# Two attention blocks and two Fourier blocks on one core: a job's projection, second norm and MLP placed among the attention steps of the next job

## The chip, the cores and the metric

The kernel runs on one core of one Trainium2 chip. The metric is device time in microseconds (us) from the start to the end of the one launch, taken as the median of several runs; lower is better.

## The reference, cut to what matters

Four blocks follow one another on an image batch of 8 x 16 x 16 x 192 (batch, height, width, channels), all in float32. The first two are windowed attention blocks with an MLP (the window is 14 x 14 and the image is padded to 28 x 28, so each image has four windows, three of them mostly padding). The last two go through the Fourier domain.

```
h = layernorm(x) * w + b                      # over the 192 channels
q, k, v = split(windows(h) @ qkv_w + qkv_b)   # 12 heads of 16 channels
a = (q / 4) @ k.T + rel_h(q) + rel_w(q)       # relative position terms, by row and by column
o = softmax(a) @ v
x = x + unwindow(o @ proj_w + proj_b)
h = layernorm(x) * w2 + b2
x = x + gelu(h @ up_w + up_b) @ down_w + down_b      # 192 -> 768 -> 192
# blocks 3 and 4
x = x + irfft2(softshrink(mix2(relu(mix1(rfft2(x))))))   # block-diagonal complex mixes
```

## The kernel before, in words

**Jobs, units and steps.** The batch is cut into four pairs of images (512 tokens each) and the two attention blocks are two layers, which makes eight *jobs*, numbered n = 0 to 7: job n is pair n % 4 in layer n // 4. A job's attention has nine *units* (three groups of four heads, times three kinds of windows: the full windows of image one, those of image two, and the cut ones, which the code calls window 2), and a unit has four heads, so a job has 36 *steps*. In a step TensorE makes the scores of a head that is some steps ahead (`scores`, L829), VectorE takes the row maximum (`row_max`, L435), and, for the head of this step, TensorE makes the transposed scores with the maximum already subtracted (`scores_T`, L869), ScalarE takes the exponential (`exps`, L617). The maxima of a unit are transposed on TensorE (`transpose_max`, L855), copied on VectorE (`copy_max`, L448) and put into a row of `q_aug` by a DMA that ScalarE issues (`send_max`, L660; two DMAs for a full window, one for a cut one). Once a unit's four exponentials are there, `values` (L885) multiplies them with v.

**The front of a job** is what comes before its attention: the first norm's transposes `transpose_x` (x), the projections to q and k in two groups of six heads, g = 0 and 1 (`project`, q and k), the relative terms (`bias`, 16 small matmuls, and `transpose_bias`, for each group and each axis; the program calls them h, H, w, W) and v (`values_in`). Each result is split into a high and a low part: ScalarE writes the high part (`q_high`, `k_high`, `r_high`), then VectorE the low one (`q_low`, `k_low`, `r_low`). Then SyncE (SP) sends them into the rows of `q_aug` and `k_aug` by DMAs within SBUF: for each group of six heads four of 192 KB for q, four of 192 KB for k, four of 168 KB for the relative terms (`send_keys` L238, `send_queries` L251, `send_bias` L258, and the loop `send` L275).

**The back of a job** is what follows its attention: transposes of the attention's output (`transpose_out`), the output projection (`project_out`), the residual sum and second norm on VectorE and GpSimd, `transpose_y`, the MLP's first product in six blocks (`up`, L939), gelu on ScalarE (L655), the second product (`down`, L951) and the sum to x. Gelu and exp need different tables of ScalarE: a dummy activation (`warm`, L673) makes the switch at a place of the program's choice.

**Order.** Every engine's program is written out by hand and runs in order. In the main loop over units u and heads e the 36 steps hold `scores` 12 heads ahead, `scores_T`, `values`, and group 0 of the next job's front at fixed steps (`X_SLOT`, `Q_SLOT`, `K_SLOT`, `R_SLOT`). After the 36 steps comes a stretch without steps: group 1 of the next front and the back of this job, in turns; the first 12 `scores` of the next job stand between the matmuls of `down`. In this document A is the stretch from the first to the last exponential of a job, and B the stretch from there to the first exponential of the next job.

**Banks.** PSUM has eight banks. Banks 0 and 1 hold scores, 2 and 3 transposed scores, 4 the values, 5 the small transposes, and 6 and 7 the front, in turns: the list `FRONT` gives each use its bank, and `front_free` (L755) makes TensorE wait until the use two places earlier has been read. The back uses banks 0 to 4, as no attention runs then. The MLP's hidden values lie in the memory of the exponentials `PT`. The weights of both layers have their own memory, loaded early.

Of the kernel before, what the change touches and what calls it, by code (L numbers as in the profile page):

```python
# [11 lines left out]
PAIRS = B // 2  # L12
# [15 lines left out]
RK = WS * HG  # L28
MLP = 4 * C
# [7 lines left out]
HEADS = 4 * UNITS  # L37
EARLY = 12
LAST = UNITS - 1
# [4 lines left out]
INV = [1.0 / 16, 1.0 / 256]  # L44

# [9 lines left out]
def window(u):  # L55
    return u % 3


def slot(n, u):
    return (UNITS * n + u) % 4  # L60


def head(i):
    return 4 * (i // 12) + i % 4
# [6 lines left out]
def front_uses(n):  # L71
    uses = ["x0", "x1", "q0", "k0"]
    if first_of_layer(n):
        uses += ["p0"]
    uses += ["h0", "H0", "w0", "W0", "q1", "k1"]
    if first_of_layer(n):
        uses += ["p1"]
    return uses + ["h1", "H1", "w1", "W1", "v0", "v1", "v2", "v3"]


FRONT = [(n, use) for n in range(JOBS) for use in front_uses(n)]
PROJ_BANK = (0, 1, 4, 2)
UP_BANK = (4, 3)
DOWN_BANK = (2, 4, 3, 2)
X_SLOT, Q_SLOT, K_SLOT, R_SLOT = 3, 8, 12, (18, 24)
BIAS_ORDER = ("h a w", "w h a")
V_TILES = [(0, 1), (2, 3), (4, 5), (6,)]


def front_bank(n, use):  # L90
    return 6 + FRONT.index((n, use)) % 2

# [33 lines left out]
def attention(nc, d, x_all, bank, consts):  # L126
    with ExitStack() as ctx:
# [3 lines left out]
        def sem(name):  # L131
# [6 lines left out]
        w_proj = [sb(f"w_proj{l}", [97, G, C]) for l in range(2)]  # L138
        w_up = [sb(f"w_up{l}", [96, G, MLP]) for l in range(2)]
        w_down = [sb(f"w_down{l}", [128, MC, C]) for l in range(2)]  # L140
        b_up = [sb(f"b_up{l}", [128, MC]) for l in range(2)]
        b_down = [sb(f"b_down{l}", [128, C]) for l in range(2)]
# [24 lines left out]
        spare = sb("spare", [1, 2])  # L167
        hidden = PT[:, :, :].rearrange("p s m -> p (s m)")[:, 0:MC * TOK].rearrange("p (m k) -> p m k", m=MC)
# [8 lines left out]
        PER = dict(stats1=1, stats2=1, aggr1=1, aggr2=1, veps1=1, veps2=1, rstd1=1, rstd2=1, xn1=1, xn2=1, xT_mm=2,  # L177
                   xT_dve=1, xT_act=1, q_mm=2, q_hi=2, q_lo=2, q_nat=2, k_mm=2, k_hi=2, k_lo=2, r_tok=4, rt_copy=4, r_mm=4, r_hi=4, r_lo=4,
                   v_mm=4, v_copy=4, s_mm=HEADS, max=HEADS, nt_mm=UNITS, negT=UNITS, st_mm=HEADS, exp=HEADS,
                   pv=UNITS, o_copy=UNITS, ot_mm=3, inv_sum=3, o_tok=3, oT_mm=2, oT_dve=1, oT_act=1, proj=4, x1=4, x1b=1,  # L180
# [9 lines left out]
        q_in = [sem(f"q_in{g}") for g in range(G)]  # L190
        k_in = [sem(f"k_in{g}") for g in range(G)]
        p_in = [sem(f"p_in{g}") for g in range(G)]
# [4 lines left out]
        Q_DMA, K_DMA, P_DMA = 16 * 8, 16 * 4, 16 * 4  # L197
        LD_FRONT, LD_BACK, LD_STATIC = 16 * 4, 16 * 7, 16 * 3

        def need(eng, name, n, k):  # L200
            if n >= 0:
                eng.wait_ge(S[name], n * PER[name] + k)

        def neg_count(n, u):
            U = UNITS * n + u
            return 16 * sum(1 if window(k % UNITS) == 2 else 2 for k in range(U % 4, U + 1, 4))

        def columns(u):
            return (CUT0, CUT) if window(u) == 2 else (WIN * window(u), WIN)
# [5 lines left out]
        def _(sp):  # L215
# [13 lines left out]
            def load_back(l):  # L229
                load(w_proj[l][0:96, :, :], d["proj_w"][l].rearrange("(g p) n -> p g n", g=G), ld_back[l])  # L230
                load(w_proj[l][96:97, 0, :], d["proj_b"][l].rearrange("(a n) -> a n", a=1), ld_back[l])
                load(b_down[l][:, :], d["down_b"][l].rearrange("(a n) -> a n", a=1).broadcast_to([128, C]), ld_back[l])
                load(b_up[l][:, :], d["up_b"][l], ld_back[l])
                load(w_up[l][:, :, :], d["up_w"][l].rearrange("(g p) n -> p g n", g=G), ld_back[l])
                load(w_down[l][:, 0:3, :], d["down_w"][l].rearrange("(g p) n -> p g n", g=MC)[:, 0:3, :], ld_back[l])
                load(w_down[l][:, 3:6, :], d["down_w"][l].rearrange("(g p) n -> p g n", g=MC)[:, 3:6, :], ld_back[l])

            def send_keys(n, g):  # L238
                need(sp, "st_mm", n - 1, 4 * (6 if g == 0 else UNITS))
                need(sp, "k_lo", n, g + 1)  # L240
                for z in range(2):
                    for r in (z, z + 2):
                        load(k_aug[r:BIAS:4, HG * g:HG * g + HG, 0:TOK].bitcast(F32), st_k[:, g, z, :].bitcast(F32), k_in[g])
                if first_of_layer(n):
                    sp.wait_ge(S["p_lo"], 2 * layer(n) + g + 1)
                    for z in range(2):
                        for r in (z, z + 2):
                            load(k_aug[r:BIAS:4, HG * g:HG * g + HG, TOK:KEYS].bitcast(F32),
                                 st_p[:, g, z, :].bitcast(F32), p_in[g])

            def send_queries(n, g):  # L251
                need(sp, "st_mm", n - 1, 4 * (6 if g == 0 else UNITS))
                need(sp, "q_lo", n, g + 1)
                for z in range(2):
# [28 lines left out]
            for n in range(JOBS):  # L283
                if n + 1 < JOBS:
                    send(n + 1)
                if n == 0:
                    load_front(1)
# [1062 lines left out]
```

## Time and profile before

| what | value |
|---|---|
| timed runs: median (lowest to highest, three runs) | 833.28 us (831.12 to 837.92) |
| profiled execution: span from first to last instruction | 836.0 us |
| TensorE busy | 721.2 us (86%) |
| TensorE weight loads busy (beside the matmuls) | 524.7 us (63%) |
| VectorE, ScalarE, GpSimd busy | 360.0, 341.1, 114.9 us |
| mean granted TensorE clock, as a share of 2.4 GHz | 0.879 |
| first exponential of job 0, last of job 7 | 54.65 us, 694.3 us |
| first fold of the Fourier blocks | 738.2 us |

The profile gives the profiled execution no other time than its span; nothing is listed around it, and the span lies between the lowest and the highest timed run. Busy times are sums over the span. A row's time in the timeline runs from its start to its (modelled) end, and neighbouring TensorE rows may overlap by the length of the array's pipeline. A granted clock of 1.00 is 2.4 GHz and one of 0.50 is 1.2 GHz; values between are means of the two. DMA issues are not counted as busy time of the engine that issues them.

### The profile page before, as it was taken

The numbers are of one execution on the slowest core, as the hardware profiler recorded it, in microseconds if no ns is written. First come the engines' busy times: TensorE is split into PE (matmuls) and PEld (weight loads), VectorE is DVE, ScalarE is ACT, GpSimd is POOL, SyncE is SP. The second block draws the span as 40 slices with busy tenths as digits, with TensorE's granted clock in tenths as the row PEclk, the third lists the DMA queues.
The fourth block names the chain that finished last, engine by engine and source line by source line (L and its number), as shares of the span: only waits on it lengthen the run. The fifth ranks groups of instructions, "written<-read, shape, count | busy, mean of one in ns | idle before, by whom it ended". The sixth has DMA issues, their size and how long they took to land. (4 is left out here: it accounts for less than half of the span.)

```text
span 836.0 us, 14490 instructions
## 1 busy us (share of the span) xinstructions
PE 721.2 (86%) x5592; PEld 524.7 (63%) x5592; DVE 360.0 (43%) x977; ACT 341.1 (41%) x813; POOL 114.9 (14%) x161
## 2 busy tenths in 40 slices
PE   3799879998998899879988897899898886979996
PEld 1476557666676567656765575567665765567664
DVE  3275235514362427441744273417421642046664
ACT  3335433543255244534353445243533352225443
POOL 3120030001200220022002200220001000023331
PEclk9778899857997799898989999789768985789999
DMA  7931630055105420360036005400341000000000
GB/s 191 182 66 28 135 85 2 3 114 145 29 2 110 106 62 2 83 149 18 2 70 138 12 2 110 94 16 2 78 110 32 2 3 0 1 1 20 20 20 19
DMA packets 32937, 47.30 MB, mean 57 GB/s; under 512 B 5452, under 2 KB 13966, under 8 KB 32870
## 3 DMA queue, kind: packets, MB, share of 16 engines
q1 hardware_dynamic: 31910, 46.18, 23.9%
q8 instruction: 45, 0.74, 0.4%
q10 hardware_dynamic: 960, 0.20, 0.1%
q14 instruction: 22, 0.18, 0.1%
HBM read 7.05 MB, written 1.57 MB: 10 GB/s over the span
## 5 line engine op out<-in xcount | busy, mean ns | idle before, releaser
L626 ACT ACTIVATE PT<-bank 98x392 f32<-98x392 f32 (+1 forms) x288 | 137.3, 490 | 177.1 <-PE bank L881 165.1
L444 DVE TENSOR_REDUCE neg_max<-bank 98x2 f32<-98x392 f32 x192 | 104.2, 561 | 114.1 <-PE bank L851 113.1
L881 PE MATMUL bank<-q_aug,k_aug 127*98 127x196 f32 (+1 forms) x672 | 124.8, 291 | 18.6 <-ACT PT L626 6.8
L881 PEld LDWEIGHTS bank<-q_aug,k_aug 127*98 127x98 f32 (+1 forms) x672 | 99.5, 195 | 37.8 <-issue 18.8
L947 PE MATMUL bank<-yT,w_up 96*128 96x512 f32 x192 | 87.4, 613 | 7.9 <-ACT yT L652 7.9
L851 PE MATMUL bank<-k_aug,q_aug 126*98 126x196 f32 x384 | 87.3, 310 | 2.5 <-DVE neg_max L444 1.8
L791 PE MATMUL bank<-xT,w_qkv 96*96 96x512 f32 (+2 forms) x144 | 87.0, 729 | 1.4 <-ACT xT L567 1.4
L957 PE MATMUL bank<-w_down,PT 128*128 128x192 f32 x384 | 78.2, 331 | 6.2 <-ACT PT L657 6.2
L320 POOL TENSOR_TENSOR q_nat<-st_q 96x392 f32<-96x392 f32 (+2 forms) x48 | 24.8, 544 | 412.9 <-DVE st_q L412 412.9
L897 PE MATMUL bank<-PT,v_aug 98*32 98x196 f32 (+1 forms) x1344 | 74.1, 355 | 0.9 <-ACT o_nat L642 0.9
L825 PE MATMUL bank<-w_qkv,xT 97*98 97x192 f32 (+1 forms) x224 | 56.5, 417 | 20.7 <-DVE st_r L432 20.7
L947 PEld LDWEIGHTS bank<-yT,w_up 96*128 96x128 f32 x192 | 37.0, 196 | 54.3 <-issue 52.9
L957 PEld LDWEIGHTS bank<-w_down,PT 128*128 128x128 f32 x384 | 61.1, 191 | 12.8 <-ACT PT L657 12.8
L851 PEld LDWEIGHTS bank<-k_aug,q_aug 126*98 126x98 f32 x384 | 55.8, 169 | 15.0 <-DVE neg_max L444 6.1
L825 PEld LDWEIGHTS bank<-w_qkv,xT 97*98 97x98 f32 (+1 forms) x224 | 47.9, 223 | 25.2 <-DVE st_r L432 23.0
L657 ACT ACTIVATE PT<-bank,b_up 128x512 f32<-128x512 f32 x48 | 33.0, 687 | 59.9 <-PE bank L947 59.9
L847 PE MATMUL bank<-k_aug,q_aug 126*120 126x318 f32 x96 | 45.4, 475 | 12.9 <-DVE neg_max L444 12.5
L897 PEld LDWEIGHTS bank<-PT,v_aug 98*32 98x32 f32 (+1 forms) x1344 | 40.1, 125 | 22.0 <-issue 10.7
L442 DVE TENSOR_REDUCE neg_max<-bank 120x1 f32<-120x318 f32 x96 | 45.2, 484 | 12.6 <-PE bank L847 12.0
L432 DVE TENSOR_TENSOR st_r<-bank,st_r 84x392 fp32r<-84x392 f32 (+2 forms) x96 | 26.0, 323 | 53.5 <-ACT st_r L605 53.5
L313 POOL TENSOR_TENSOR rstd<-veps,half_pow 128x4 f32<-128x4 f32 x16 | 16.4, 1024 | 197.7 <-DVE veps L367 197.7
L791 PEld LDWEIGHTS bank<-xT,w_qkv 97*96 97x96 f32 (+1 forms) x144 | 25.5, 203 | 25.8 <-issue 24.6
(87 smaller groups left out, 888.9 us busy)
## 6 DMA issues: line engine op xcount, KB each, us to landing
q_aug<-st_q SPq DMA_DIRECT2D x64, 192.0 KB
k_aug<-st_k SPq DMA_DIRECT2D x64, 192.0 KB, 4.6
q_aug<-st_r SPq DMA_DIRECT2D x64, 168.0 KB
x_all<-in_x SPq DMA_DIRECT2D x4, 384.0 KB, 6.8
q_aug<-negT ACTq DMA_DIRECT2D x96, 1.5 KB
out<-y_out SPq DMA_DIRECT2D x4, 384.0 KB, 2.6
k_aug<-st_p SPq DMA_DIRECT2D x16, 74.2 KB, 4.2
w_up<-in_up_w SPq DMA_DIRECT2D x2, 576.0 KB
```

The lines of the kernel that those rows point to most:

```text
L442: ins = v.tensor_reduce(neg_max[0:CUT, slot(n, u), e:e + 1], b[0:CUT, 0:CUT + PADS], AX.X, ALU.max, negate=True)
L444: ins = v.tensor_reduce(neg_max[0:HALF, slot(n, u), e:e + 5:4], b[0:HALF, 0:2 * WIN] .rearrange("p (r m) -> p r m", r=2), AX.X, ALU.max, n ...
L626: s.activation(PT[0:rows, i % 8, 0:m], bank[2 + i % 2][0:rows, 0:m], ACT.Exp).then_inc(S["exp"], 1)
L657: s.activation(hidden[:, f, :], bank[UP_BANK[f % 2]][:, :], ACT.Gelu, bias=b_up[layer(n)][:, f:f + 1])\
L791: ins = t_.matmul(b[0:96, 0:cols[1] - cols[0]], w_qkv[l][0:rows, part, c0 + 96 * g:c0 + 96 * g + 96], xT[0:rows, part, cols[0]:cols[1]], s ...
L825: last = t_.matmul(b[0:rows, C * k:C * k + C], xT[0:97 - g, g, c0:c0 + rows], w_qkv[l][0:97 - g, g, 2 * C:3 * C], start=(g == 0), stop=(g ...
L847: last = t_.matmul(b[0:CUT, 0:CUT + PADS], q_aug[0:NEG, h, c:c + m], k_aug[0:NEG, h, c:KEYS], start=True, stop=True)
L851: last = t_.matmul(b[0:HALF, WIN * r:WIN * r + WIN], q_aug[0:NEG, h, c + HALF * r:c + HALF * r + HALF], k_aug[0:NEG, h, c:c + WIN], start= ...
L881: last = t_.matmul(b[0:keys, m * k:m * k + m], k_aug[0:NEG + 1, h, c + keys * k:c + keys * k + keys], q_aug[0:NEG + 1, h, c:c + m], start= ...
L897: last = t_.matmul(bank[4][32 * e:32 * e + 32, c:c + m], v_aug[0:rows, t0 + k, head(i), :], PT[0:rows, i % 8, m * k:m * k + m], start=(k = ...
L947: last = t_.matmul(bank[UP_BANK[f % 2]][:, :], w_up[l][:, g, 128 * f:128 * f + 128], yT[0:96, g, :], start=(g == 0), stop=(g == 1))
L957: ins = t_.matmul(bank[DOWN_BANK[t]][:, 0:C], hidden[:, f, 128 * t:128 * t + 128], w_down[l][:, f, :], start=(f == 0), stop=(f == MC - 1))
```

## The change: what it does

Three things change together.

**The back moves into the steps of the next job.** The loop over jobs m has 36 steps k. At fixed steps TensorE, VectorE and ScalarE do, beside the step's attention of job m, a piece of the back of job m - 1 and a piece of the front of job m + 1 (both groups now). There is no stretch without steps any more, but for the back of job 7 at the end. `scores` run 8 heads ahead (`LEAD`), across the border of jobs.

**All of it shares banks 6 and 7.** The list `FREE` gives the uses of the front and the back one order and turns; the wait is again for the use two places earlier. `hidden` has memory of its own; to make room the back's weights have one copy, and those of layer 1 are loaded over those of layer 0 (`load_back(1)`, issued in the SP program behind the sends of job 5).

**Sends by pairs of heads.** The channels of q, k and the relative terms are ordered by pairs of heads, and SP sends a pair at a time: 12 DMAs of 64 KB (56 KB for the relative terms) for each of six pairs, 72 for a job where there were 24. Pairs 0 and 1 are sent once 12 steps of the job before are over, pairs 2 and 3 once 24 are, pairs 4 and 5 once all 36 are.

```
+STEPS = 4 * UNITS
+LEAD = 8
+V_AT = (35, 0, 1, 2)
+X_AT = 3
+Q_AT, K_AT = (5, 15), (7, 16)
+B_AT = ((9, 13), (18, 22))
+BT_AT = ((10, 14), (21, 25))
+P_AT = (29, 30)
+O_AT = 8
+PROJ_AT = (11, 12)
+Y_AT = 17
+UP_AT = (19, 20, 23, 24, 27, 28)
+DOWN_AT = (31, 32, 33, 34)
...
+def free_bank(n, use):
+    return 6 + FREE.index((n, use)) % 2
...
             def load_back(l):
+                if l:
+                    need(sp, "proj", PAIRS - 1, 2)
+                load(w_proj[0:96, :, :], d["proj_w"][l].rearrange("(g p) n -> p g n", g=G), ld_back[l])
...
+            def send(n, pairs_of_heads, done):
+                need(sp, "st_mm", n - 1, done)
+                for j in pairs_of_heads:
+                    send_queries(n, j)
+                for j in pairs_of_heads:
+                    send_keys(n, j)
+                for axis in range(2):
+                    for j in pairs_of_heads:
+                        send_bias(n, j, axis)
...
+            send(0, (0, 1, 2), 0)
+            send_all_pads(0, (0, 1, 2))
+            send(0, (3, 4, 5), 0)
+            send_all_pads(0, (3, 4, 5))
+            for m in range(JOBS):
+                if m + 1 < JOBS:
+                    send(m + 1, (0, 1), 12)
+                    send(m + 1, (2, 3), 24)
+                    send_all_pads(m + 1, (0, 1, 2, 3))
+                    send(m + 1, (4, 5), STEPS)
+                    send_all_pads(m + 1, (4, 5))
...
+                if m == PAIRS:
+                    load_back(1)
...
         @block.scalar
...
+            for m in range(JOBS):
+                more, past = m + 1 < JOBS, m >= 1
+                for k in range(STEPS):
+                    U, e = UNITS * m + k // 4, k % 4
+                    exps(STEPS * m + k)
+                    if e == 1 and U + 1 < UNITS * JOBS:
+                        send_max(U + 1)
+                    if e == 2 and U >= 1:
+                        copy_o(U - 1)
...
+                        if k in UP_AT[1::2]:
+                            warm(ACT.Gelu)
+                            f = UP_AT.index(k)
+                            gelu(m - 1, f - 1)
+                            gelu(m - 1, f)
+                            warm(ACT.Exp)
...
         @block.tensor
...
+            def scores(s):
+                U, e = s // 4, s % 4
+                n, h = U // UNITS, head(U, e)
+                if window(U) == 0 and e % 2 == 0:
+                    for landed in (q_in, k_in, r_in):
+                        pe.wait_ge(landed[h // 2], SENT * (n + 1))
...
+                need_all(pe, "max", s - 1)
...
+            for m in range(JOBS):
+                more, past = m + 1 < JOBS, m >= 1
+                for k in range(STEPS):
+                    U, e = UNITS * m + k // 4, k % 4
+                    if STEPS * m + k + LEAD < STEPS * JOBS:
+                        scores(STEPS * m + k + LEAD)
+                    if e == 0 and U + 1 < UNITS * JOBS:
+                        transpose_max(U + 1)
+                    scores_T(STEPS * m + k)
+                    if e == 1 and U >= 1:
+                        values(U - 1)
...
+                        if k in UP_AT:
+                            up(m - 1, UP_AT.index(k))
+                        if k in DOWN_AT:
+                            down(m - 1, DOWN_AT.index(k))
```

The order of uses of banks 6 and 7 within the loop of a job m is: v1 v2 v3 of job m; x0 x1 q0 k0 of job m + 1; t0 t1 (the output's transposes) of job m - 1; h0 H0 (m + 1); o0 o1 (projection, m - 1); w0 W0 q1 k1 (m + 1); y0 y1 (m - 1); h1 (m + 1); u0 u1 (up, m - 1); H1 w1 (m + 1); u2 u3 (m - 1); W1 (m + 1); u4 u5, d0 to d3 (down, m - 1); v0 (m + 1).

ScalarE, before, in stretch B of a job: the last splits of the front, the switch to the table of gelu (`spare` is the dummy's tile), six gelus, the switch back, and the sends of the next job's first maxima (`st_r` relative terms, `yT` the MLP's input, the first `PT` rows are gelu's output, the last exponentials).

```order
L605 ACTIVATE st_r<-bank 84x64
L614 ACTIVATE v_aug<-bank 98x24x16 x2
L614 ACTIVATE v_aug<-bank 106x24x16
L674 ACT_TABLE_LOAD
L674 ACTIVATE spare<-spare 1x1
L652 ACTIVATE yT<-bank,affine 96x512
L614 ACTIVATE v_aug<-bank 106x12x16
L657 ACTIVATE PT<-bank,b_up 128x512 x6
L674 ACT_TABLE_LOAD
L674 ACTIVATE spare<-spare 1x1
L669 DMA q_aug<-negT 1x4x98 x4
L626 ACTIVATE PT<-bank 98x392 x3
```

ScalarE now, steps 20 to 22 of a job with a back to do (`PT` are exponentials, `hidden` gelu's output, `negT` the maxima that are sent):

```order
L713 ACTIVATE PT<-bank 106x360
L759 ACT_TABLE_LOAD
L759 ACTIVATE spare<-spare 1x1
L741 ACTIVATE hidden<-bank,b_up 128x512 x2
L759 ACT_TABLE_LOAD
L759 ACTIVATE spare<-spare 1x1
L713 ACTIVATE PT<-bank 106x360
L753 DMA q_aug<-negT 1x4x98 x2
L695 ACTIVATE st_r<-bank 84x392
L695 ACTIVATE st_r<-bank 84x56
L695 ACTIVATE st_r<-bank 84x64
L713 ACTIVATE PT<-bank 106x360
```

The six gelus have become three pairs, each with a switch to gelu's table and one back, and they stand between the exponentials of steps 20 and 21, 24 and 25, 28 and 29; the send of maxima and the split of the front's relative terms stand behind them.

TensorE, before, around the MLP's first product in stretch B (`xn` transposes, the last of v, then `up`, then `down` with `scores` between):

```order
L825 MATMUL bank<-w_qkv,xT 106x192 x4
L936 MATMUL bank<-ident,xn 96x128 x8
L825 MATMUL bank<-w_qkv,xT 106x192 x2
L947 MATMUL bank<-yT,w_up 128x512 x12
L957 MATMUL bank<-w_down,PT 128x192 x2
L851 MATMUL bank<-k_aug,q_aug 98x196 x2
L957 MATMUL bank<-w_down,PT 128x192 x2
```

TensorE now, from the second block of `up` in step 20 to the third in step 23 (`L930` is `scores`, `L954` `scores_T`, `L968` `values`, `L897` the transposes H1, `L887` the relative terms w1, `L1019` `up`):

```order
L1019 MATMUL bank<-yT,w_up 128x512 x2
L930 MATMUL bank<-k_aug,q_aug 98x196 x2
L954 MATMUL bank<-q_aug,k_aug 106x120 x3
L968 MATMUL bank<-PT,v_aug 32x196 x8
L897 MATMUL bank<-ident,rt 84x128 x4
L930 MATMUL bank<-k_aug,q_aug 98x196 x2
L954 MATMUL bank<-q_aug,k_aug 106x120 x3
L887 MATMUL bank<-w_rel,q_nat 32x84 x16
L930 MATMUL bank<-k_aug,q_aug 98x196 x2
L954 MATMUL bank<-q_aug,k_aug 106x120 x3
L1019 MATMUL bank<-yT,w_up 128x512 x2
```

Between two blocks of `up` there are now up to three steps of attention and pieces of the front; before, the twelve matmuls of `up` stood in one row.

## Rows read from the trace of the kernel before

**Rows 1.** The page: its first line, TensorE's in part 1, the clock in 40 slices.

```profile
span 836.0 us, 14490 instructions
...
PE 721.2 (86%) x5592; PEld 524.7 (63%) x5592; DVE 360.0 (43%) x977; ACT 341.1 (41%) x813; POOL 114.9 (14%) x161
...
PEclk9778899857997799898989999789768985789999
```

**Rows 2.** Busy time by stage: stretch, its us, busy us of PE PEld DVE ACT POOL, clock, DMA.

```profile
443.12:486.90 43.78, 37.95 (x268) 27.97 (x267) 19.21 (x57) 14.01 (x31) 9.38 (x10) 1.00 0.25 54
486.90:522.67 35.77, 30.39 (x368) 22.69 (x367) 17.74 (x45) 22.08 (x59) 1.56 (x3) 0.98 0.31 65
...
54.65:662.98 608.33, 542.29 (x4442) 396.36 (x4443) 259.32 (x708) 254.91 (x611) 71.52 (x86) 0.88 0.26 60
662.98:694.30 31.32, 27.69 (x279) 20.51 (x277) 14.06 (x34) 17.94 (x46) 0.00 (x0) 0.86 0.01 2
```

**Rows 3.** Timeline of TensorE in B of job 4: start us, us, line, operation.

```profile
447.40 0.79 PE L805 MATMUL bank<-w_rel,q_nat 96*32 96x84 f32 x32
...
449.09 0.60 PE L815 MATMUL bank<-ident,rt 128*84 128x128 f32 x4
...
463.67 10.54 PE L947 MATMUL bank<-yT,w_up 96*128 96x512 f32 x24 [1.32 <-ACT yT L652]
...
477.32 0.48 PE L851 MATMUL bank<-k_aug,q_aug 126*98 126x196 f32 x2
477.63 0.83 PE L957 MATMUL bank<-w_down,PT 128*128 128x192 f32 x4
```

**Rows 4.** Timeline of TensorE in A of job 5.

```profile
488.94 0.42 PE L851 MATMUL bank<-k_aug,q_aug 126*98 126x196 f32 x2
...
489.39 0.34 PE L851 MATMUL bank<-k_aug,q_aug 126*98 126x196 f32 x2
...
489.85 0.87 PE L897 MATMUL bank<-PT,v_aug 98*32 98x196 f32 x16
```

**Rows 5.** Timeline of all engines in A of job 5, around step 18.

```profile
505.67 0.71 ACT L605 ACTIVATE st_r<-bank 84x392 fp32r<-84x392 f32 x3 [0.81 <-PE bank L815]
...
506.41 0.81 DVE L432 TENSOR_TENSOR st_r<-bank,st_r 84x392 fp32r<-84x392 f32 x3 [1.66 <-ACT st_r L605]
...
507.75 0.41 PE L847 MATMUL bank<-k_aug,q_aug 126*120 126x318 f32 x1 [1.78 <-DVE neg_max L444]
```

**Rows 6.** Timeline of ScalarE: a table switch in B of job 4, a send in A.

```profile
474.24 0.69 ACT L657 ACTIVATE PT<-bank,b_up 128x512 f32<-128x512 f32 x1 [1.03 <-PE bank L947]
474.95 1.28 ACT L674 ACT_TABLE_LOAD   x1
476.24 0.20 ACT L674 ACTIVATE spare<-spare 1x1 f32<-1x1 f32 x1
...
509.86 0.47 ACT L626 ACTIVATE PT<-bank 106x360 f32<-106x360 f32 x1 [0.95 <-PE bank L881]
509.87 1.20 ACTq L669 DMA_DIRECT2D q_aug<-negT  x2
...
511.11 0.47 ACT L626 ACTIVATE PT<-bank 106x360 f32<-106x360 f32 x1 [0.78 <-PE bank L881]
```

**Rows 7.** Busy time by stretch, as in rows 2, where the clock changes.

```profile
160.60:163.00 2.40, 0.62 (x5) 0.49 (x5) 1.54 (x6) 1.68 (x6) 0.00 (x0) 1.00 0.01 1
163.00:190.00 27.00, 26.56 (x187) 16.42 (x187) 4.80 (x13) 10.02 (x27) 1.54 (x3) 0.50 0.50 107
...
201.00:208.00 7.00, 6.72 (x26) 6.12 (x27) 0.65 (x3) 1.72 (x3) 1.39 (x1) 0.54 0.49 127
```

**Rows 8.** SP's sends for job 0, its first scores, and the page's time to landing.

```profile
22.13 2.55 SPq L217 DMA_DIRECT2D q_aug<-st_q  x4
...
29.88 3.44 SPq L217 DMA_DIRECT2D q_aug<-st_r  x4
...
46.73 0.67 PE L851 MATMUL bank<-k_aug,q_aug 126*98 126x196 f32 x4
...
k_aug<-st_k SPq DMA_DIRECT2D x64, 192.0 KB, 4.6
```

More of the change, by code:

```diff
@@ L28 @@
 RK = WS * HG
+SUB = HG // 2
 MLP = 4 * C
@@ L52, in pair, with window, head, free_bank_uses @@
     return n % PAIRS
[L55 to L64, printed above, removed]
+def window(U):
+    return U % 3
+def head(U, e):
+    return 4 * (U % UNITS // 3) + e
 def first_of_layer(n):
     return n % PAIRS == 0
[L71 to L91, printed above, removed]
+def free_bank_uses():
+    uses = []
+    def front(n, wanted):
+        uses.extend((n, use) for use in wanted.split())
+    pads = lambda n, use: use if first_of_layer(n) else ""
+    front(0, "x0 x1 q0 k0 p0 h0 H0 w0 W0 q1 k1 p1 h1 H1 w1 W1 v0")
+    for m in range(JOBS + 1):
+        now, more, past = m < JOBS, m + 1 < JOBS, m >= 1
+        if now:
+            front(m, "v1 v2 v3")
+        if more:
+            front(m + 1, "x0 x1 q0 k0")
+        if past:
+            front(m - 1, "t0 t1")
+        if more:
+            front(m + 1, "h0 H0")
+        if past:
+            front(m - 1, "o0 o1")
+        if more:
+            front(m + 1, "w0 W0 q1 k1")
+        if past:
+            front(m - 1, "y0 y1")
+        if more:
+            front(m + 1, "h1")
+        if past:
+            front(m - 1, "u0 u1")
+        if more:
+            front(m + 1, "H1 w1")
+        if past:
+            front(m - 1, "u2 u3")
+        if more:
+            front(m + 1, "W1")
+        if past:
+            front(m - 1, "u4 u5")
+        if more:
+            front(m + 1, pads(m + 1, "p0 p1"))
+        if past:
+            front(m - 1, "d0 d1 d2 d3")
+        if more:
+            front(m + 1, "v0")
+    return uses
+FREE = free_bank_uses()
+def free_bank(n, use):
+    return 6 + FREE.index((n, use)) % 2
 def pieces(x, y, order="a h w"):
@@ L229, in load_back @@
             def load_back(l):
[L230 to L234, printed above, removed]
@@ L557, in _ @@
+            last = JOBS - 1
+            divide(3 * JOBS - 1)
+            copy_oT(last)
+            add_proj(last, 0)
+            second_stats(last, 0)
+            add_proj(last, 1)
+            second_stats(last, 1)
+            normalise(last)
+            place_y(last)
+            for t in range(TILES):
+                add_mlp(last, t)
         @block.scalar
@@ L688, in _ @@
                     r_high(0, g, a)
-            for j in range(4):
-                copy_v(0, j)
+            copy_v(0, 0)
             act.wait_ge(static, 2)
@@ L749, in _ @@
+            last = JOBS - 1
+            copy_o(UNITS * JOBS - 1)
+            warm(ACT.Gelu)
+            copy_oT(last)
+            place_y(last)
+            for f in range(MC):
+                gelu(last, f)
+            for U in range(UNITS * JOBS - 4, UNITS * JOBS):
+                act.wait_ge(neg_in[U % 4], neg_count(U))
         @block.tensor
@@ L1059, in channels @@
+            last_job = JOBS - 1
+            values(UNITS * JOBS - 1)
+            transpose_o(3 * JOBS - 1)
+            transpose_out(last_job)
+            for k in range(2):
+                project_out(last_job, k)
+            transpose_y(last_job)
+            for f in range(MC):
+                up(last_job, f)
+            for t in range(TILES):
+                down(last_job, t)
 def channels(f, p, a):
```

847 lines of the change are left out of this document (383 added, 464 removed).

## The prediction, made before the changed kernel ran

> **What bounds the kernel now.** I read the page first. TensorE is busy for 86% of the span, far more than any other engine, at a granted clock whose forty digits change between 5 and 9 [rows 1]. So the kernel is bound by TensorE, and two things stand above its work: its idle time and its clock. Then I cut the span into stages [rows 2]. From the first exponential of job 0 to that of job 7 there are seven job periods in 608.33 us, 86.9 us each, with TensorE busy for 542.29 / 7 = 77.5 at a mean clock of 0.88. One period that ran at nearly full clock (B of job 4 with A of job 5) took 43.78 + 35.77 = 79.6 us with TensorE busy for 37.95 + 30.39 = 68.3. So of the mean period 68.3 us are work, 11.2 us are waits, and 86.9 - 79.6 = 7.3 us are what the lower clock costs. The profiled execution ends 836.0 - 694.3 = 141.7 us after the last exponential; this end (the back of job 7 and the Fourier blocks) the change leaves as it is. The span stands 2.7 us above the median of the runs (833.28) and within them, so I sum against the span and take 2.7 off at the end.
>
> The timelines tell what the waits are. In A, TensorE waits on chains through other engines: 1.78 us for a maximum that stands on VectorE behind the split of the relative terms, ScalarE 0.71 and VectorE 0.81 each [rows 5]. In B it waits on the chain of the back (norm, copies, gelu).
>
> **Part 1: the back among the steps.** What goes is B as a stretch in which the back's chains have no attention beside them: if all 11.2 us went, a job would take 68.3. TensorE's work stays; I take 67, as a few ends of isolated groups get covered. What comes is a set of new waits.
>
> Steps 8 to 14 place the output's transposes and the projection between pieces of the front whose banks must be read first: k_low, the copy of the relative terms, a maximum behind r_low as in [rows 5], each about 0.6. Four of them: 2.4.
>
> Steps 20 to 31 are the ones that matter, since ScalarE switches its table six times there, before each pair of gelus and after it. I walk the first pair from the end of step 19's up block. A step of scores and transposed scores takes 0.45 and values 0.87 [rows 4]; an up block 10.54 / 6 = 1.76, the transposes H1 0.60, the relative terms w1 0.79 [rows 3]. ScalarE: exponential 20 ends at 1.2, the table is in at 1.2 + 1.28 + 0.20 = 2.7, two gelus of 0.69 end at 4.1, the table is back at 5.6, exponential 21 (0.47) ends at 6.1, the two sends of maxima hold the queue for 1.20 to 7.3, the split of H1 ends at 8.0 on ScalarE and, with 0.81, at 8.9 on VectorE [rows 5, 6]. TensorE has step 20, up block 1, step 21, values, H1, step 22 and w1 behind it at 0.45 + 1.76 + 0.45 + 0.87 + 0.60 + 0.45 + 0.79 = 5.4. Then the transposed scores of step 23 want exponential 21 and wait about 0.8; the third up block wants the bank of H1, which is read at 8.9, where TensorE stands at 6.4: 2.5. Queued behind that block are all scores of step 24 on, and VectorE and ScalarE wait for these. The second pair costs by the same walk 1.4 (exponential 25) and 1.2 (the next unit's maxima), the third 1.6. Together 7.5. A count agrees: ScalarE has 12 exponentials (5.6), three sends (3.6), six loads with spare (8.9), six gelus (4.1), splits and copies (some 3.4), 25.6 us in these steps, and TensorE 21.2. So the stretch is ScalarE's.
>
> The Trainium skill, "ScalarE: Activation LUTs", section "What ACT_TABLE_LOAD costs", puts a switch at some 1283 ns for the load and about 1380 ns of drain, and "Table sets: the hidden batching unit" advises batching by set, which speaks against three pairs. Here the load takes 1.28 but starts 0.02 us after the gelu before it ends [rows 6], so no drain is in my walk.
>
> At full clock a job thus takes 67 + 2.4 + 7.5 = 76.9.
>
> **Part 2: the clock.** The clock fell to 0.50 at 163 for 27 us after 2.40 us in which TensorE was busy for 0.62 only, and stood near 0.5 again from 201 to 208, with TensorE full [rows 7]; it stayed at 1.00 and 0.98 in B of job 4 and A of job 5 [rows 2]. The change takes away the longest idle stretches but adds waits of 1 to 2.5 us. The bounds are 0 and the 7.3 us of now. The waits left (9.9) are nearly as many as before (11.2) but in shorter pieces than that 1.8 us of idle, so I take half, 3.5. A job is 80.4, six of them 482.4.
>
> **Part 3: sends by pairs.** A send's issue holds SP for 2.55 / 4 = 0.64 (q) or 3.44 / 4 = 0.86 (relative terms) at 192 or 168 KB [rows 8]. At a third of the size no row shows it on SP. If the price goes with the bytes it is a third, 0.21 and 0.29. If it goes with the count it stays; ScalarE pays 1.20 / 2 = 0.60 for a send of one row [rows 6]. That is the nearest row for a small send, and I take 0.64 and 0.86. A job's 72 sends are 48 x 0.64 + 24 x 0.86 = 51 us of SP, within 80, and each pair has more than 15 steps from issue to use, so they stay hidden in the steady state.
>
> Not in job 0. Before its first exponential SP issues, from 22.1 on, three pairs' q, k and relative terms and the pads (for each 12 DMAs), then the same of the other three: 96 sends, 66 us. The first three pairs' relative terms are out at 22.1 + 12 x 0.64 + 12 x 0.64 + 12 x 0.86 = 47.8; pair 0 lands about when the first scores run now (46.73), so I put the first exponential at 53.5, about a microsecond earlier than now because only one of four v blocks stands ahead of it. Pair 3's relative terms are issued at some 77 and land 2.6 later (64 KB take less than the 4.6 us of 192 KB [rows 8]). Its first scores stand in step 6 (14 - 8), where TensorE comes at about 65. So it waits some 14 us, once. The other 30 steps of job 0 have work for 33.6 (67 less the back's 24 is 43; the first six steps did 9.4), waits 7, clock 3; A of job 0 ends at 123.4, 69.9 us after it began. By the price per byte there is no wait, 14 less; with 0.86 for all of them it is some 14 more.
>
> **Part 4: one copy of the back's weights.** The load for layer 1 stands on SP behind the 24 sends of job 5's last two pairs (17 us, from the start of job 5) and the projection of job 4 wants it in step 11, some 20 us in. Seven loads and their landing make it late by 5 (3 to 8), once.
>
> **Part 5: job 7.** A of job 7 now holds the back of job 6: its work 48.2 (24 of attention, 27.69 busy at 0.86 now [rows 2], and 24 of a back: 10.5 for up and 6.5 for down [rows 3], the rest transposes and projection, an estimate), waits 10, clock 3.5, and 1.5 for the maxima at its end: 63, where A takes 31.3 now [rows 2].
>
> **Sum.** 53.5 + 69.9 + 482.4 + 5 + 63 + 141.7 = 815.5, which is 20.5 less than 836.0; on the median 813. VectorE and GpSimd have no more work than before and are covered. A job of 83.8 would be even with now: 3.4 us above the forecast.
>
> **The rivals.**
> - A, the clock stays full: TensorE hardly idles, each of eight jobs loses the 3.5, and sends cost by bytes (14 less). 815.5 - 28 - 14 = 773. For it: B and A ran at 1.00 and 0.98 [rows 2]. Against: 0.54 with TensorE full [rows 7].
> - B, the clock costs what it does now: 3.8 x 7 = 27 more, 842 in the span, 840 on the median: no change.
> - C, slower: the ScalarE stretch takes the place of B. Steps 20 to 31 leave TensorE some 7.5 us idle in 29; if the clock drops there as it did at 163, the four remaining up blocks (7.0) and the downs (6.5) run at half speed, some 6 more after what overlaps ScalarE and 3 in the steps behind them, of which the 3.5 covers 3. That is 6 a job, 42 in seven: 857 in the span, 855 on the median. It decides from 83.8 a job on. For it: 25.6 of ScalarE against 21.2, and the fall behind an idle stretch [rows 7]. Against: single waits are under 2.5 us.
>
> By the Trainium skill's drain (page above) six switches cost up to 6 x 1.38 = 8.3 us more a job, about 7 after cover, an estimate that ends near 862, on C's side; the trace so far speaks against it [rows 6].
>
> **How the numbers follow.** Forecast 0.44, A 0.17, B 0.17, C 0.22. A measurement of this kernel tells about 1% from no change, which puts the borders at 825 and 841.6. Faster holds the forecast and A but for a few per cent: 0.60. Within 1% holds most of B: 0.16. Slower holds C and B's upper part: 0.24. The range goes from A's 774 to just above C's, 858; the forecast's own is 800 to 826 (the 14 us of part 3 one way, half the clock term the other).
>
> **What would show it.** Right: six table loads in steps 20 to 31 of each job and TensorE's wait before the third up block; periods near 80 us; 0.6 us per 64-KB send; scores waiting at step 6 of job 0 till about 79; a wait at the projection of job 4 alone. Clock digits of 9 throughout speak for A, the same as now for B, fives in the second half of every job for C. The forecast is wrong if a period is above 83.8, or if the sends of pairs 2 to 5 are late in every job.

## The result and the profile after

The changed kernel takes 763.39 us (median of four runs, 758.59 to 766.09) against 835.6 (831.12 to 843.04): a ratio of 0.912, interval 0.905 to 0.920. That is 72 us less where 20 were forecast, and below the low end of the range (774). The prediction had the direction right and missed the size.

The page of the changed kernel, its first line, TensorE's, and the clock in 40 slices:

```profile
span 763.4 us, 15089 instructions
...
PE 650.4 (85%) x5592; PEld 486.9 (64%) x5592; DVE 351.1 (46%) x961; ACT 369.8 (48%) x869; POOL 114.9 (15%) x161
...
PEclk9977699999999999999999889999999996989998
```

Beside [rows 1] the surprise is what did not change: TensorE is busy for 85% of the span after 86%, and its idle time over the whole run is 763.4 - 650.4 = 113.0 us after 836.0 - 721.2 = 114.8. Its busy time fell by 70.8 us for the same 5592 matmuls. The digits of the clock, nearly all 9, give the larger part: by the clock records of the two traces the time at half the clock (a granted clock of 0.50) fell from 202.0 to 92.9 us, which is worth about half the difference, an estimate of 55 us. The other 16 fit matmuls that overlap more (66.3 us of work in an undisturbed job, below, for 68.3 in the fast period before). And the unchanged total of idle time hides a shift: jobs 1 to 6 idle 25 us less, job 0 idles 12 more (it waits for its sends), the start, the A of job 7 and the end together 11 more.

Now the stages, as in [rows 2]: from the first exponential of job 0 to that of job 1, job 1 to 2, job 2 to 3, job 5 to 6, then all seven periods, the A of job 7, and the end:

```profile
56.05:127.77 71.72, 49.42 (x503) 37.65 (x503) 28.54 (x76) 27.68 (x73) 8.11 (x11) 0.81 0.33 77
127.77:198.00 70.23, 66.29 (x635) 50.41 (x634) 35.77 (x101) 40.45 (x97) 10.94 (x13) 1.00 0.33 79
198.00:269.77 71.77, 67.96 (x635) 51.20 (x634) 35.77 (x101) 40.46 (x97) 10.93 (x13) 0.98 0.28 65
412.14:495.35 83.21, 71.12 (x635) 54.26 (x634) 35.95 (x101) 40.29 (x97) 10.93 (x13) 0.90 0.31 73
56.05:565.60 509.55, 456.59 (x4309) 346.80 (x4309) 242.43 (x669) 270.58 (x645) 68.68 (x84) 0.95 0.31 74
565.60:624.47 58.87, 52.09 (x436) 39.82 (x434) 23.69 (x63) 32.59 (x72) 2.84 (x2) 0.97 0.11 26
624.47:763.40 138.93, 113.97 (x644) 84.05 (x644) 64.61 (x175) 52.06 (x124) 28.53 (x51) 0.91 0.04 12
```

An undisturbed job takes 70.2 us at full clock: 66.3 of work and 3.9 of waits. Job 5 is 13 us longer, for a reason of its own (the wait of 8.4 us below). The sum of the stages against before, in us: first exponential +1.4, job 0 -15.5 (87.2 to 71.7), jobs 1 to 6 -83.3 (521.1 to 437.8), A of job 7 +27.6, the end -2.8; together -72.6.

What TensorE waits for in job 1 (the columns are the waiting and the awaited instruction, us in total, times, the longest), and the two largest waits that the change added, in jobs 0 and 5:

```profile
PE bank L954 <- ACT PT L713: 2.3, 2, 1.3
PE bank L1019 <- DVE st_r L513: 0.9, 1, 0.9
PE bank L987 <- DVE st_k L498: 0.2, 1, 0.2
PE bank L897 <- issue: 0.2, 1, 0.2
PE bank L941 <- DVE neg_max L525: 0.2, 1, 0.2
...
PE bank L930 <- DMA q_aug<-st_r: 15.6, 1, 15.6
...
PE bank L1000 <- DMA w_down<-in_down_w: 8.4, 1, 8.4
```

And the stretch that the prediction walked, the first pair of gelus (steps 20 to 23 of job 1), in the timeline; compare [rows 6]:

```profile
163.00 1.94 PE L1019 MATMUL bank<-yT,w_up 96*128 96x512 f32 x4
163.19 0.47 ACT L713 ACTIVATE PT<-bank 106x360 f32<-106x360 f32 x1 [1.76 <-PE bank L954]
163.68 1.28 ACT L759 ACT_TABLE_LOAD   x1
165.09 0.66 ACT L741 ACTIVATE hidden<-bank,b_up 128x512 f32<-128x512 f32 x1
165.40 0.58 ACTq L753 DMA_DIRECT2D q_aug<-negT  x1
165.66 0.66 ACT L741 ACTIVATE hidden<-bank,b_up 128x512 f32<-128x512 f32 x1
166.02 0.58 ACTq L753 DMA_DIRECT2D q_aug<-negT  x1
166.34 1.28 ACT L759 ACT_TABLE_LOAD   x1
167.74 0.44 ACT L713 ACTIVATE PT<-bank 106x360 f32<-106x360 f32 x1
168.09 0.67 ACT L695 ACTIVATE st_r<-bank 84x392 fp32r<-84x392 f32 x3
168.23 0.49 PE L954 MATMUL bank<-q_aug,k_aug 127*106 127x120 f32 x3
168.79 0.82 DVE L513 TENSOR_TENSOR st_r<-bank,st_r 84x392 fp32r<-84x392 f32 x3 [3.07 <-ACT st_r L695]
169.66 0.70 PE L1019 MATMUL bank<-yT,w_up 96*128 96x512 f32 x1 [0.94 <-DVE st_r L513]
```

The two sends of maxima stand in ScalarE's program behind exponential 21 (167.74), and they are issued at 165.40 and 166.02, beside the gelus. So ScalarE issued them here while its arithmetic was still some instructions behind, and the gelus, the load and the exponential follow one another without a gap. In [rows 6] the two sends did delay the next exponential: its scores in the kernel before,

```profile
509.86 0.41 PE L881 MATMUL bank<-q_aug,k_aug 127*106 127x120 f32 x3
```

were done by 510.27, and it began at 511.11, just after the sends (509.87 + 1.20). There ScalarE had no earlier arithmetic left that could run meanwhile.

### The profile page after: what moved, and what is told of

Same layout as the page of the kernel before. It is cut to its first block and busy times, and to the rows that moved or that the text cites. A ratio compares the mean times of both kernels' runs of the same rounds, so it can differ in the third digit from the quotient of the medians.

```text
span 763.4 us, 15089 instructions
## 1 busy us (share of the span) xinstructions
PE 650.4 (85%) x5592; PEld 486.9 (64%) x5592; DVE 351.1 (46%) x961; ACT 369.8 (48%) x869; POOL 114.9 (15%) x161
## 5 line engine op out<-in xcount | busy, mean ns | idle before, releaser
L954 PE MATMUL bank<-q_aug,k_aug 127*98 127x196 f32 (+1 forms) x672 | 115.2, 265 | 17.9 <-ACT PT L713 16.8
L930 PE MATMUL bank<-k_aug,q_aug 126*98 126x196 f32 x384 | 99.2, 342 | 25.4 <-DMA q_aug<-st_r 15.6
L954 PEld LDWEIGHTS bank<-q_aug,k_aug 127*98 127x98 f32 (+1 forms) x672 | 90.3, 173 | 26.2 <-ACT PT L713 19.7
L1019 PE MATMUL bank<-yT,w_up 96*128 96x512 f32 x192 | 99.7, 649 | 6.6 <-DVE st_r L513 5.6
L930 PEld LDWEIGHTS bank<-k_aug,q_aug 126*98 126x98 f32 x384 | 57.3, 172 | 62.3 <-issue 56.1
L873 PE MATMUL bank<-xT,w_qkv 96*96 96x512 f32 (+3 forms) x144 | 69.5, 611 | 1.9 <-ACT xT L653 1.4
L1028 PE MATMUL bank<-w_down,hidden 128*128 128x192 f32 x384 | 68.9, 331 | 1.0 <-ACT hidden L741 0.9
L1028 PEld LDWEIGHTS bank<-w_down,hidden 128*128 128x128 f32 x384 | 61.7, 190 | 4.2 <-issue 2.2
L968 PE MATMUL bank<-PT,v_aug 98*32 98x196 f32 (+1 forms) x1344 | 63.0, 312 | 0.6 <-ACT PT L713 0.6
L1019 PEld LDWEIGHTS bank<-yT,w_up 96*128 96x128 f32 x192 | 35.7, 204 | 36.3 <-issue 28.5
L759 ACT ACT_TABLE_LOAD x43 | 55.2, 1283 | 0.8
L568 DVE TENSOR_TENSOR x_all<-bank,x_all 128x192 f32<-128x192 f32 x32 | 11.4, 358 | 77.6 <-PE bank L1028 77.6
L907 PE MATMUL bank<-w_qkv,xT 97*98 97x192 f32 (+1 forms) x224 | 44.2, 338 | 0.0
L968 PEld LDWEIGHTS bank<-PT,v_aug 98*32 98x32 f32 (+1 forms) x1344 | 34.3, 110 | 11.2 <-ACT PT L713 1.0
```

Source lines behind the costliest of these rows:

```text
L759: s.activation(spare[:, at:at + 1], spare[:, 0:1], function)
L873: ins = t_.matmul(b[0:96, 0:cols[1] - cols[0]], w_qkv[l][0:rows, part, c0 + 96 * g:c0 + 96 * g + 96], xT[0:rows, part, cols[0]:cols[1]], s ...
L907: last = t_.matmul(b[0:rows, C * k:C * k + C], xT[0:97 - g, g, c0:c0 + rows], w_qkv[l][0:97 - g, g, 2 * C:3 * C], start=(g == 0), stop=(g ...
L930: last = t_.matmul(b[0:HALF, WIN * r:WIN * r + WIN], q_aug[0:NEG, h, c + HALF * r:c + HALF * r + HALF], k_aug[0:NEG, h, c:c + WIN], start= ...
L954: last = t_.matmul(b[0:keys, m * k:m * k + m], k_aug[0:NEG + 1, h, c + keys * k:c + keys * k + keys], q_aug[0:NEG + 1, h, c:c + m], start= ...
L968: last = t_.matmul(bank[4][32 * e:32 * e + 32, c:c + m], v_aug[0:rows, t0 + k, head(U, e), :], PT[0:rows, (4 * U + e) % 8, m * k:m * k + m ...
```

## The experiments

Four questions: does ScalarE set the time of the stretch with the table switches; which part of the change gains; why is the clock so much better; and can the waits that are left go. On the clock there are three theories: theory 1 is that single long waits pull it down, theory 2 that it goes its own way, theory 3 that it follows the idle time of a job, however cut.

**Without the table switches.** This kernel leaves gelu out in every job but the last (the hidden values are the first product and its bias) and with it the switches of `warm`:

```diff
-                s.activation(hidden[:, f, :], bank[free_bank(n, f"u{f}")][:, :], ACT.Gelu, bias=b_up[:, f:f + 1])\
+                s.activation(hidden[:, f, :], bank[free_bank(n, f"u{f}")][:, :], ACT.Gelu if n == JOBS - 1 else ACT.Identity, bias=b_up[:, f:f + 1])\
...
-                            warm(ACT.Gelu)
...
-                            warm(ACT.Exp)
```

> The six table loads of every job but the last go: gelu is left out there (the hidden values are the first product and its bias). By the walk of the prediction (the stretch of steps 20 to 31 is ScalarE's and costs 7.5 us a job) seven jobs lose 52 us: about 711. By the waits that the trace shows there (0.9 + 1.3 + 1.0 a job) at most 22 us, and up to 8 of clock: 733 to 745.

Measured: 731.37 us (span 729.6, 34 below the changed kernel's). Job 1 of that kernel, and its two waits:

```profile
128.42:194.65 66.23, 65.57 (x635) 50.21 (x634) 35.74 (x101) 32.61 (x84) 10.92 (x13) 1.00 0.35 83
...
PE bank L985 <- DVE st_k L498: 0.2, 1, 0.2
PE bank L939 <- DVE neg_max L525: 0.2, 1, 0.2
```

Switches and gelus together cost 70.2 - 66.2 = 4.0 us a job, not 7.5; the three waits of the stretch (3.2) are gone, and with them nearly all idle time. It came out just below the lower of the two ranges, as A of job 7 gained 6.9 by itself (58.9 to 52.0).

**Two more sends in the stretch.**

```diff
+                    if U % UNITS in AGAIN:
+                        for r in range(2):
+                            act.dma_start(aside[0:1, U % UNITS - 6, r, :, :].bitcast(F32),
+                                          negT[4 * r:4 * r + 4, U % 4, 0:8].bitcast(F32))\
+                                .then_inc(neg_in[U % 4], 16)
```

> In units 6 and 7 of each job ScalarE issues two more small sends behind those of the maxima (32 values each to a spare place), behind the exponentials of steps 21 and 25, where it is late. By the walk of the prediction (a send holds ScalarE for 0.6 us) 2 x 1.2 = 2.4 us a job, 19 us in eight: about 782. If ScalarE issues a send while earlier activations still run, as the trace of the changed kernel shows beside the gelus: 0 to 4 us more, 763 to 767.

Measured: 767.56 us, 4 above the changed kernel (span 765.7, 2.3 above), at the upper edge of the 0 to 4 expected if sends are free and far from the 19 of the walk. Job 1 took 70.18 us after 70.22. The added pair in job 1, in the timeline of ScalarE:

```profile
168.59 1.28 ACT L766 ACT_TABLE_LOAD   x1
168.89 1.19 ACTq L760 DMA_DIRECT2D aside<-negT  x2
169.89 0.20 ACT L766 ACTIVATE spare<-spare 1x1 f32<-1x1 f32 x1
170.00 0.44 ACT L715 ACTIVATE PT<-bank 106x360 f32<-106x360 f32 x1
```

The 1.19 us begin inside the table load and end 0.2 after it, beside the dummy of the switch, and the exponential follows the load as before (1.41 us from the load's start to it, 1.40 without the added sends). The sends are free there: shown.

**The back in one piece.** All of the back of job m - 1 stands at step 17; the turns of banks 6 and 7 follow the new order, and the six gelus have one switch and one back. TensorE's part of the edit:

```diff
+                        if k == Y_AT:
                             transpose_out(m - 1)
...
+                            for j in range(2):
+                                project_out(m - 1, j)
                             transpose_y(m - 1)
...
+                            for f in range(MC):
+                                up(m - 1, f)
+                            for t in range(TILES):
+                                down(m - 1, t)
```

> The back of the last job stands in one piece at step 17, no step of attention between its parts; the front stays spread, sends by pairs stay, and the six gelus have one switch and one back. If spreading the back is what gained: its chains lie open again (before: waits of 2.96 and 1.3 us in the back, and the table load and gelus at its end), some 6 to 8 us of idle and 3 to 5 us of clock a job, seven jobs: 63 to 90 us more, 826 to 853. If the front in the steps and the sends gained it, or six loads fewer weigh it up: within 15 us of 763.

Measured: 883.76 us, ratio 1.047 (1.034 to 1.059) to the kernel before. Its waits in job 2, and job 1's period:

```profile
PE bank L974 <- DVE xn L450: 4.3, 1, 4.3
...
PE bank L983 <- ACT yT L703: 1.0, 1, 1.0
PE bank L964 <- ACT yT L698: 0.9, 1, 0.9
PE bank L992 <- ACT hidden L708: 0.9, 1, 0.9
...
126.54:217.31 90.77, 77.66 (x634) 57.87 (x633) 36.67 (x102) 36.12 (x88) 10.91 (x13) 0.86 0.26 62
```

The chain of the second norm alone is 4.3 us of open wait. So one switch in place of three does not make up for it, and the front in the steps without the back loses to the kernel before, where the front's second half stood between the pieces of the back. With the rest of the change as it is, spreading the back is what gains. Undoing it cost more than the 63 to 90 us expected, 882.0 - 763.4 = 118.6, and the excess is mostly in the clock: by the table further down (21.6 - 4.0) / 2 = 8.8 us a job for the 3 to 5 expected, and 13.8 - 5.1 = 8.7 of idle time for 6 to 8.

**Sends by groups again.**

```diff
-                    send(m + 1, (0, 1), 12)
-                    send(m + 1, (2, 3), 24)
+                    send(m + 1, (0, 1, 2), 24)
...
-                    send(m + 1, (4, 5), STEPS)
+                    send(m + 1, (3, 4, 5), STEPS)
```

> The changed kernel, with the small sends of jobs 1 to 7 gathered by groups again: pairs 0 to 2 after step 24, pairs 3 to 5 after step 36 of the job before. If the sending by pairs is needed for the gain: pair 3's relative terms are issued behind 24 sends of 0.64 and eight of 0.86, some 22 us into the job, and wanted at step 4, some 8 us in: 14 to 16 us of wait a job and the clock behind it (as behind the 15.6 us wait of job 0: 17 us at half, 8.5 lost), seven jobs: 100 to 165 us more, 865 to 930. If the queue has slack for it: 763.

Measured: 977.7 us, ratio 1.167. One line of its waits:

```profile
PE bank L929 <- DMA q_aug<-st_r: 209.4, 15, 21.2
```

The time is above the 865 to 930 expected: two waits a job came of it, where I had counted one. The three dates of sending are a condition of the gain. The 64-KB size by itself was not tried.

**One wait, three waits.** To see what idle time does to the clock, GpSimd holds TensorE in jobs 0 to 6, once behind step 33 or in three pieces behind steps 31, 33 and 35 (`HELD_AT` gives step and number of dummy operations):

```diff
+                    for j, (at, _) in enumerate(HELD_AT):
+                        if k == at and m < JOBS - 1:
+                            pe.wait_ge(held, len(HELD_AT) * m + j + 1)
```

> The changed kernel, with TensorE held behind step 33 of jobs 0 to 6 until GpSimd has done three dummy operations of about 1 us. Theory 1: seven waits of 3 us, and behind each a stretch of some 7 us at half the clock as behind the 2.96 us waits of the kernel before: 7 x (3 + 3.4) = 45 us more, about 808. Theory 2: 21 us more, about 784.

> The same three dummy operations, one each behind steps 31, 33 and 35. Theory 1: the same idle time in pieces of 1 us leaves the clock nearly alone (0.94 us waits in the changed kernel had a half-clock stretch of 3.4 us behind them in some jobs, none in others): 21 us of waits and 0 to 12 of clock, 784 to 796, at least 12 us faster than with one wait. Theory 2: as with one wait, about 784.

> As the run with one wait of three dummy operations, with six (a wait of about 6.1 us once in jobs 0 to 6, some 10 us of idle a job, as much as the kernel before had). Theory 3 (the clock follows how much TensorE idles in a job, however cut): some 20 us at half a job as in the kernel before, 9 lost: 7 x (6.1 + 9) = 106 more than the changed kernel, about 869. Theory 1 in its milder form (each long wait takes a stretch of its own, 8.4 us of wait had 13.7 at half behind it): 7 x (6.1 + 5 to 7) = 78 to 92 more, 841 to 855. Idle time alone: 43 more, 806.

> Two dummy operations behind each of steps 31, 33 and 35: three waits of some 2.1 us a job. Theory 3: as with one long wait, about 869. Theory 1 in its milder form (a wait of 1.8 to 3 us had 3.4 to 6.8 us at half behind it): 7 x (6.3 + 3 x 1.7 to 3.4) = 80 to 115 more, 843 to 878, so no better than one long wait. Idle time alone: 44 more, 807.

Measured: 797.48, 799.79, 823.05 and 840.14 us. No theory's number was met: the first lies between theory 2 (784) and theory 1 (808), the third between idle time alone (806) and theory 1's milder form (841), the second and the fourth 3 to 4 us off theory 1's. Job 2 of each, in that order:

```profile
212.03:287.10 75.07, 68.04 (x635) 52.07 (x634) 35.83 (x101) 40.47 (x97) 13.89 (x16) 0.98 0.26 62
```

```profile
212.36:287.99 75.63, 68.46 (x635) 51.32 (x634) 35.77 (x101) 40.43 (x96) 13.96 (x16) 0.98 0.26 62
```

```profile
216.64:294.86 78.22, 68.16 (x635) 51.75 (x634) 35.77 (x101) 40.51 (x97) 16.84 (x19) 0.96 0.25 60
```

```profile
220.57:302.57 82.00, 71.78 (x634) 54.29 (x634) 35.83 (x101) 40.61 (x96) 16.93 (x19) 0.94 0.24 57
```

Here are the means over jobs 1 to 6, worked out from the traces: period, idle time of TensorE, and time at half the clock, in us.

| kernel | period | idle | at half |
|---|---|---|---|
| no switch | 68.1 | 2.1 | 1.7 |
| changed | 73.0 | 5.1 | 4.0 |
| one wait of 3.1 | 77.4 | 8.4 | 5.8 |
| three of 1.1 | 77.7 | 8.5 | 5.7 |
| one of 6.1 | 81.1 | 11.1 | 9.8 |
| three of 2.1 | 83.1 | 10.7 | 11.4 |
| before | 86.9 | 9.3 | 21.0 |
| back in one piece | 89.9 | 13.8 | 21.6 |

One profile stands behind each row. The kernel before has a mean clock of 0.879 in its profile and of 0.863 to 0.920 in 23 other runs, so its row is near the middle of what it does. From "no switch" to "three of 2.1" the means hold job 5 with its wait for weights; without that job idle and half-clock time are 3.7 and 1.4 in the changed kernel, 9.8 and 7.6, 10.1 and 10.5 in the two with most idle time, and 9.0 and 21.9 before.

Theory 2 falls: in the mean, though not in every single job, the added waits brought time at half the clock with them, the more the longer they were. Theory 1 as first put falls too: at 3 us in all, one wait or three made no difference. Twice as much idle time cost more than its own length, in three pieces more (77 us in the time) than in one (60). Theory 3 fails by its number: with at least as much idle time as the kernel before, the two kernels with 6 us of waits added spent about half as long at half the clock. So less idle time explains part of the better clock; what else in the kernel before, beside the amount of idle time, held the clock down stays open.

**Towards a faster version.** First the two waits that the change added: job 0 sends two pairs at a time, and the load of the projection's weights has its own place and semaphore.

```diff
+            for some in ((0, 1), (2, 3), (4, 5)):
+                send(0, some, 0)
+                send_all_pads(0, some)
...
+                    if m == PAIRS:
+                        load_proj(1)
                     send(m + 1, (2, 3), 24)
```

> Job 0's sends go two pairs of heads at a time, and the load of the projection's weights for layer 1 is issued after step 12 of job 4 with a semaphore of its own. Theory 1 (a single long wait of TensorE pulls its clock down behind it, and what the change gained over the forecast is that no job has one any more): the waits of 15.6 us (job 0) and 8.4 us (job 5) go, and with them the half-clock stretches of 17.1 and 13.7 us behind them, which cost half their length: 763 - 24 - 15 = about 724 us. Theory 2 (the clock goes its own way, the gain is covered work only): only the waits go, about 739 us, and half-clock stretches as long stand elsewhere.

Measured: 743.7 us (span 740.4, clock 0.963). The wait in job 5 is gone with its half-clock stretch. In job 0 the waits for relative terms are 14.5 us in three pieces, as SP comes late to the next sends too, so the 24 us of waits went only in part:

```profile
PE bank L935 <- DMA q_aug<-st_r: 14.5, 3, 9.5
```

Theory 2's number (739) lies nearer than theory 1's (724), but jobs 1 to 6 now have no time at half the clock (4.0 us in the mean in the changed kernel), where theory 2 wanted as much as before.

Then the order of steps 18 to 30, on top of that:

```diff
-B_AT = ((9, 13), (18, 22))
-BT_AT = ((10, 14), (21, 25))
+B_AT = ((9, 13), (18, 21))
+BT_AT = ((10, 14), (22, 30))
...
-UP_AT = (19, 20, 23, 24, 27, 28)
+UP_AT = (19, 20, 23, 24, 26, 28)
```

> The kernel of the first run (its 740.4 us span), with the pieces of steps 18 to 30 in another order: w1 at 21 and H1 at 22, the fifth up block at 26, W1 at 30. If the 3.2 us of waits a job in steps 20 to 31 come from where work stands and not from too much work of ScalarE: two of the three go, about 2 us a job in seven: 724 to 730. If the stretch is ScalarE's, as the prediction has it, the waits move and the time stays at 738 to 744.

Measured: 734.41 us. Job 1, and its three largest waits:

```profile
122.90:191.90 69.00, 66.41 (x635) 50.50 (x634) 35.75 (x101) 40.43 (x96) 10.97 (x13) 1.00 0.35 84
...
PE bank L955 <- ACT PT L714: 0.9, 2, 0.6
PE bank L942 <- DVE o_tok L545: 0.6, 1, 0.6
PE bank L942 <- DVE neg_max L526: 0.5, 2, 0.3
```

Of the 3.2 us of waits for exponentials and the split 0.9 is left, with the same six loads, but waits of 0.6 and 0.3 for VectorE came up beside them: 1.8 us of waits are left in these steps. So somewhat under half of the waits came of the order alone; whether a better order would take the rest, which the kernel without switches does not have, was not tried. The gain of 9 us is below the 10 to 16 expected, as the idle time of a job fell by 1.5 only (4.0 to 2.5 in the mean of jobs 1 to 6).

Last, on top of both, ScalarE sends job 0's pads in place of SP:

```diff
+            send_pads(0)
+            send_pads(1)
             send_max(0)
...
+                    if m == 0 and k in PADS_AT:
+                        send_pads(2 + PADS_AT.index(k))
```

> The kernel of the run before, and job 0's pads sent by ScalarE in place of SP, so that SP comes 15 us earlier to the relative terms: the waits of 3.5, 1.5 and 9.5 us in job 0 go, and half of the 17 us at half the clock behind them: 14 to 22 us less than the run before.

Measured: 727.28 us, ratio 0.870 (0.864 to 0.877): the fastest of the study. Job 0 lost 9.6 us (74.4 to 64.8), but its first exponential came at 50.7, against 48.5 in the run before and 51.3 in the first of these three (those two have the same program up to there, so the start itself varies by 3 us). The gain is 7 us in all, half of the low end of what I expected. Whether ScalarE's sends delay that start is not settled by this.

## Why the prediction was wrong, by its own steps

Of the 52.1 us by which the span was forecast too long (815.5 to 763.4), 49.6 are in jobs 1 to 6 (482.4 + 5 to 437.8). The other stages missed by less and in both directions: the first exponential came 2.5 us later than forecast, job 0 took 1.8 more, A of job 7 4.1 less, the end 2.8 less. That these nearly cancel is luck.

- **What bounds the kernel**: right as to TensorE and the two things above its work, mis-sized as to the clock. I set idle 11.2 and clock 7.3 a job, the idle time of the one fast period for all. The mean period of jobs 1 to 6 has 9.3 idle and 21.0 at half, which costs about 10.5.
- **Part 1, the walk**: this is the step that failed: it priced the waits of a job at 9.9 us, and an undisturbed job has 3.9. These 6.0 are most of the 8.2 us by which a job was too long (the rest is 1.5 of clock and 0.7 of work). "The two sends of maxima hold the queue for 1.20" put the split of H1 and the third up block behind them; they ran beside the gelus, and the block waited 0.94 in place of 2.5. The bank of H1 was read 7.1 us after the walk's start (168.79 + 0.82), where the walk had 8.9; 1.2 of the 1.8 is the sends. The walk was otherwise close: exponential 21 ended 5.6 us after the start (up block 1's start at 163.00 is 0.45 in the walk), forecast 6.1. Waits at exponential 21 (0.8) and at the maxima (1.2) did not come; those at 25 and 29 did, together 2.3 for 3.0. The waits of steps 8 to 14 (four of 0.6) shrank to three of 0.2 in job 1: I had priced each after the isolated chain of [rows 5], with nothing beside it. And the count of ScalarE's 25.6 us against 21.2 held 3.6 us of sends that take none of its time. Without them it is 22.0, nearly even. The claim that the stretch is ScalarE's falls: the kernel without switches gained 4.0 a job and not 7.5, and in the stretch ScalarE itself waits for TensorE, before exponentials 24 and 28:

```profile
172.09 0.50 ACT L713 ACTIVATE PT<-bank 98x392 f32<-98x392 f32 x1 [2.09 <-PE bank L954]
...
179.94 0.50 ACT L713 ACTIVATE PT<-bank 98x392 f32<-98x392 f32 x1 [1.27 <-PE bank L954]
```

The two engines wait for each other in turns, and the reordered kernel shows that a part of these waits hangs on the order.

- The load after a gelu again starts at once (165.66 + 0.66 to 166.34), and the profile of the changed kernel has 0.8 us of idle time before all 43 loads together:

```profile
L759 ACT ACT_TABLE_LOAD x43 | 55.2, 1283 | 0.8
```

The mean load, 1283 ns, is the figure of the Trainium skill, "ScalarE: Activation LUTs", section "What ACT_TABLE_LOAD costs"; the drain of some 1380 ns that it adds did not show.

- **Part 2, the clock**: half of 7.3, 3.5, was forecast; 4.0 us at half a job are 2.0. The direction was right. The reason given, shorter pieces of idle time, is not borne out (with 6 us of waits added, shorter pieces brought more time at half); idle time fell further than forecast, which by the added waits explains a part, and the rest is open. Against before this is 8.5 of the 13.9 us that a job gained, idle time 4.2, and the rest (1.2) work that overlaps.
- **Part 3, the sends**: right. A 64-KB send took as long as a 192-KB one, and job 0 waited 15.6 us where 14 were forecast. The first exponential came at 56.05 for 53.5.

The sends of job 0 in the timeline of SP, which answer to [rows 8]:

```profile
23.32 7.62 SPq L262 DMA_DIRECT2D q_aug<-st_q  x12
...
39.39 10.13 SPq L262 DMA_DIRECT2D q_aug<-st_r  x12
```

7.62 / 12 is 0.64, 10.13 / 12 is 0.84.

- **Part 4**: right in place, with 8.4 us just above the 3 to 8 given, and it brought time at half the clock into job 5 (17.1 us, 13.7 of them from within that wait on), which the sum did not hold. With the wait removed, job 5 had none.
- **Part 5**: 58.9 for 63; its waits came from the same walk.
- **The rivals**: A had the clock nearly right and its 773 came nearest, but by luck in part: the waits of the walk, too many by 6.0 a job, were still in it, and it had sends that cost by bytes, 14 us less, which did not come. C had its mechanism in steps 20 to 31; those waits are real but at most 1.3 us each, and behind them the clock stayed full in jobs 1, 4 and 6 and fell for 3.4 us in jobs 2 and 3. With job 0's sends and the load of weights mended and these waits as before, it stayed full in all six.

## What to carry to other kernels

Spread work with long chains between steps that do not need it, and move its transfers and their dates with it: without the spread back (883.76) or without the three dates (977.7) the kernel lost against the one before. Where TensorE is the bound, price a wait with the clock that may follow it: 3.1 us of added wait a job cost 4.9 to 5.2 here ((797.48 - 763.39) / 7 and (799.79 - 763.39) / 7). Before you add DMA issues to an engine's busy time, look in the trace whether they run beside its arithmetic.

## What was not expected of the hardware

- ScalarE issued DMAs ahead of its own queued arithmetic: two sends at 165.40 and 166.02 that stand behind an exponential of 167.74 in the program, and 1.19 us of added sends beside a table load and the dummy behind it.
- Three waits of 2.1 us a job went with more time at half the clock (11.4 us a job in the mean) than one of 6.1 (9.8).
